# A four-layer conditioned transformer kernel: the first chunk's x loads go first, from two queues, and the position load goes behind the short loads

## Chip, cores and metric

One NeuronCore of one Trainium2 chip runs the kernel. The metric is device microseconds of one execution of the whole program. The core has TensorE (PE), VectorE (DVE), ScalarE (ACT), GpSimd (POOL) and SyncE (SP); SP issues nearly all DMA transfers, and in the changed kernel ACT issues two as well.

## What is computed

The input x is 8 sequences of 256 tokens of 512 features in float32. Four layers follow: L0 (adaptive RMS norm, attention with 8 query heads and one key/value head, rotary embedding from `pos_BxS`, gated MLP), L1 (adaptive layer norm, 16-head attention on normalised q and k, GELU MLP), L2 (windowed attention with a latent key/value projection) and L3 (eight small expert MLPs, norm, projection). Only the very beginning of L0 is touched here:

```python
def ada_rms(x, t, w, tw):
    n = x * rsqrt(mean(square(x), axis=-1, keepdims=True) + EPS)
    scale = t @ tw.T
    return n * (w * (1.0 + scale))[:, None, :]

def apply_rope(x, pos_ids):
    ang = pos_ids.astype(float32)[:, :, None] * inv_freq
    ...
h = ada_rms(x, time_emb, ln1_w, ln1_tw)
q, k, v = h @ Wq.T, h @ Wk.T, h @ Wv.T      # split into heads
q, k = apply_rope(q, pos_ids), apply_rope(k, pos_ids)
```

## The kernel before, in words

The 2048 tokens are four chunks (n = 0 to 3) of 512 tokens, two sequences each. Activations lie feature-major: `X[:, c, 512n:512n+512]` is feature block c (128 partitions) of chunk n. `ORDER` lists 12 (layer, chunk) items for attention, and MLPs and tail follow the same way. Each piece of work (a norm's statistics, a projection, a softmax) is a generator in `Plan`, cut into steps; the table `PLACE` gives each step a number, and `Plan.make` sorts all steps by it. Every engine then walks the same sorted list (`weights.steps`) and issues its own part of each step, so each engine's order is fixed by `PLACE`. Engines wait on semaphores, in order, and nothing overtakes a waiting instruction on its engine.

The beginning of the list, for chunk 0 of L0, is this:

- "start" (from `PLACE["once"][0]`): SP loads the column vectors `CV` (layer weights, biases, the rotary frequencies), the four x tiles of chunk 0 (one semaphore `s_x0[c]` each), the conditioning vectors `CT` and the identity `ident`. POOL writes three constants.
- "pos" (`PLACE["trig"][0]`): SP loads the 512 positions of the chunk, broadcast to 128 partitions, into a buffer of `FB` (semaphore `s_pos`).
- "angle" (`PLACE["trig"][1]`, place 2): DVE casts the positions to float, multiplies by the frequencies and rounds to whole turns: a CAST (L372) and three TENSOR_SCALAR (L375).
- "stats" (places 3 to 8): ACT squares the four x tiles into `T` (ACTIVATE `T<-X`), DVE adds the four squares (three TENSOR_TENSOR `T<-T`, L378), PE sums over partitions (`B<-few,T`), DVE scales (`R<-B`), POOL takes the power -0.5 (`R<-R,few`).
- "load ada" 0 (place 9) loads `Y` with 1 MB of modulation weights, "load rot" (10) brings the first weight tiles `ST` and the rotation matrix; "turns" (11) is the rest of the angle work on DVE; "final" (12, 17 to 28) multiplies x by the broadcast scale and splits it into a high and a low part, `HA`. The projections `B<-HA,W` on PE start when `HA` and the split weights `W` (POOL) are there.

DVE and ACT have each one wait ahead of their whole list: `e.wait_ge(*s_cv.of())`, on the landing of `CV` (L1440, and L1755 behind one tiny activation). DVE's first instruction then waits for the positions:

```python
elif kind == "angle":
    ...
    e.wait_ge(*s_pos.of(n))
    e.wait_ge(*fr.over(gu))
    e.tensor_copy(g, f.bitcast(I32)).then_inc(*d_trig.up(n, 0))
```

Calls go through the helper class `Engine`, so the profile shows helper lines: L360 is any matmul, L363 a transpose, L366 an activation, L372 a copy or cast, L375 tensor-scalar, L378 tensor-tensor, L381 scalar-tensor-tensor, L396 a DMA.

Of the kernel before, what the change touches and what calls it, by code (L numbers as in the profile page):

```python
# [27 lines left out]
AHEAD = 2  # L28
LAG = 1
PLACE = {  # L30
    "once": [1, 10, 39, 230, 845, 943, 1214, 2226, 9, 91, 323, 400, 436, 513, 572, 614, 678, 735, 804, 848],
    "ada": [13, 14, 15, 16, 123, 147, 177, 181, 395, 396, 407, 408, 433, 434, 473, 475, 484, 486, 494, 495, 545, 546,
# [140 lines left out]
    "trig": [0, 2, 11, 29, 43, 100, 102, 136, 288, 324, 344, 404, 589, 629, 661, 704],  # L173
    "xb": [1129, 1497, 1856, 2466, 1680, 2025, 2427, 2972],
    "out": [238, 239, 240, 241, 242, 243, 244, 245, 547, 548, 549, 550, 552, 554, 555, 556, 878, 879, 880, 881, 882,
# [248 lines left out]
def span(h):  # L424

    return slice(0, 512) if h == BOTH else slice(256 * h, 256 * h + 256)
# [539 lines left out]
def program(nc, xT, pos, condT, biasd, cols, consts, tab2, wpack, adaw, out):  # L966
    ctx = ExitStack()
    with ctx:
        def sb(name, shape, dt=F32):
            return ctx.enter_context(nc.sbuf_tensor(name, shape, dt))  # L970

        def tally(name, step=1):
            return Tally(ctx.enter_context(nc.semaphore(name)), step)

        X = sb("X", [128, 4, TOK])
# [51 lines left out]
        s_x0 = [tally(f"s_x0_{c}", 16) for c in range(4)]  # L1027
# [133 lines left out]
        def left(w):  # L1161

            y = weights.before[w]
            tl, key = wused[y] if y >= 0 else (p_ada, (-1,))
            return tl.of(*key)

        def written(w):

            return s_w[weights.slot(w)].of("store", weights.before[w])
# [580 lines left out]
                    dp.done(u, d_xl, n, m, h)  # L1750

        def scalar(e):
            e.wait_ge(*g_const.of(0))
            e.activation(R16[:, 0, 0, 0:1], mhalf[:, 0:1], ACT.Square)
            e.wait_ge(*s_cv.of())  # L1755
            e.wait_ge(*g_const.of(1))
            for step in weights.steps:
# [18 lines left out]
                elif kind == "nhi":  # L1776
                    i, c, f = a
# [129 lines left out]
                elif kind == "act":  # L1907
                    q, c, j, u, f = a
# [9 lines left out]
                elif kind == "ghi":  # L1918
                    q, c, j, f = a
# [88 lines left out]
        def sync(e):  # L2008
            for step in weights.steps:
                kind, a = step[0], step[1:]  # L2010
                if kind == "start":
                    e.dma_start(CV[:, :], cols).then_inc(*s_cv.up())
                    for c in range(4):
                        e.dma_start(X[:, c, 0:512], xT[:, c, 0:512]).then_inc(*s_x0[c].up())
                    e.dma_start(CT[:, 0, :, :], condT).then_inc(*s_ct.up())
                    e.dma_start(ident[:, :], consts[0]).then_inc(*s_id.up())
                elif kind == "load rot":
                    e.dma_start(rotm[:, :], consts[1]).then_inc(*s_rot.up(0))
                elif kind == "bias":
                    e.wait_ge(*p_adt.of(ADA_GROUPS - 1))  # L2020
                    e.dma_start(BI[:, :, :], biasd.rearrange("(a p) k -> p a k", p=128)).then_inc(*s_const.up("all"))
                elif kind == "load x":
                    e.dma_start(X[:, :, 512:TOK], xT[:, :, 512:TOK]).then_inc(*s_x.up())
                elif kind == "load ada":
                    i, = a
                    e.wait_ge(*p_ada.of(i - 1))
                    e.dma_start(Y[:, :, :], adaw[:, 2048 * i:2048 * i + 2048].rearrange("p (j k) -> p j k", j=4)).then_inc(*s_ad.up(i))
                elif kind == "load":
                    w, = a
                    i, c = weights.order[w], 512 * PIECE[weights.uses[w]]  # L2030
                    if i >= STAGES:
                        tl, key = stused[i - STAGES]
                        e.wait_ge(*tl.of(*key))
                    e.dma_start(ST[:, i % STAGES, :], wpack[:, c:c + 512]).then_inc(*s_st[i % STAGES].up(w))
                elif kind == "store":
                    w, = a
                    s = weights.slot(w)
                    e.wait_ge(*g_wlo.of(w))
                    e.dma_start(kept[PIECE[weights.uses[w]]], W[:, s, :, :].bitcast(F32)).then_inc(*s_w[s].up("store", w))
                elif kind == "fetch":  # L2040
                    w, = a
                    s, name = weights.slot(w), weights.uses[w]
                    e.wait_ge(*left(w))
                    e.wait_ge(*written(w))
                    first = weights.firsts[name]
                    e.wait_ge(*s_w[weights.slot(first)].of("store", first))
                    e.dma_start(W[:, s, :, :].bitcast(F32), kept[PIECE[name]]).then_inc(*s_w[s].up("fetch", w))
                elif kind == "tables":
                    e.wait_ge(*d_qk.of("q", 0, 3, 3))
                    e.dma_start(TR[:, 0, :], tab2[0]).then_inc(*s_tab.up(0))  # L2050
                    e.dma_start(TR[:, 1, :], tab2[1]).then_inc(*s_tab.up())
                elif kind == "swap":
                    k, fu, gu = a
                    f, g, d = fr.buf(fu), fr.buf(gu), HDIM[k[1]] // 2
                    e.wait_ge(*a_raw.of(*k))
                    e.wait_ge(*fr.over(gu))
                    if k in swap_before:
                        e.wait_ge(*s_swap.of(*swap_before[k]))
                    for x in range(0, 128, 2 * d):
                        e.dma_start(g[x:x + d, :], f[x + d:x + 2 * d, :]).then_inc(*s_swap.up("part"))  # L2060
                        e.dma_start(g[x + d:x + 2 * d, :], f[x:x + d, :]).then_inc(*s_swap.up(*k))
                elif kind == "pos":
                    n, fu = a
                    e.wait_ge(*fr.over(fu))
                    e.dma_start(fr.buf(fu).bitcast(I32),
                                pos[0:1, 512 * n:512 * n + 512].broadcast_to([128, 512])).then_inc(*s_pos.up(n))
                elif kind == "ladd":
                    n, m, h, u = a
                    sp = span(h)
                    e.wait_ge(*d_xl.of(n, m, h))  # L2070
                    e.dma_start(out[:, m, 512 * n:512 * n + 512][:, sp],
                                X[:, m, 512 * n:512 * n + 512][:, sp]).then_inc(*s_out.up(n, m, h))
            e.wait_ge(*s_out.of(NB - 1, 3, 1))

        for count in (tensor, vector, scalar, gpsimd, sync):
            count(Engine())
# [5 lines left out]
        @block.sync  # L2082
        def _(eng):
            sync(Engine(eng))
# [5 lines left out]
        @block.scalar  # L2090
        def _(eng):
            scalar(Engine(eng))
# [127 lines left out]
```

## Time and profile before

| | us |
|---|---|
| median of 3 runs | 1913.11 (1912.12 to 1913.13) |
| the profiled execution | 1912.22 |
| its span | 1910.4 |
| mean granted TensorE clock | 0.987 of full speed |
| PE busy | 1839.4 (96% of the span) |

The rows further down are lines of the profile's page and of answers from its trace. A line of a timeline gives the start in us, the duration, the engine, the line of the kernel, the operation, `out<-in`, and how often it occurs in a row; in brackets the idle time before it and what ended it. SPq is SP's queue of DMA issues; the duration there is that of the issue, not of the transfer. "us to landing" is the time from the issue to the completion that the semaphore shows.

### The profile page before, as it was taken

To read this page: it belongs to the slowest core of one execution; us is meant where nothing else is said; L and a number is where in the kernel's file an instruction comes from. 1 tells how busy PE (TensorE), PEld (TensorE's weight loads), DVE (VectorE), ACT (ScalarE), POOL (GpSimd) and SP (SyncE) were. 2 spreads that over 40 slices of the span, in tenths; PEclk is the share of its full clock that TensorE was granted. 3 is DMA by queue.
4 is the path that set the end of the run, shared out by engine and by line. 5 is a ranking of instruction groups with operands and counts; after the bars stand their busy time and mean duration, and the time that the engine had idled before them with its cause. 6 is when DMAs were issued, how large, how long until landed. Compare 5 with 4: busy or idle time off the path is not lost.

```text
span 1910.4 us, 35240 instructions
## 1 busy us (share of the span) xinstructions
PE 1839.4 (96%) x12840; PEld 1480.8 (78%) x12840; DVE 1130.7 (59%) x3224; ACT 1026.9 (54%) x2482; POOL 819.3 (43%) x1094
## 2 busy tenths in 40 slices
PE   5889999999999999999999999999999999989987
PEld 3678778888888888888788888878886878865565
DVE  5867445643553446543775488586475786476563
ACT  3553433532343445443566467477467765559875
POOL 4666662211112344233778565336443442244330
PEclk9999999999999999999999999999999999989989
DMA  7436787556445544445456534623532354422421
GB/s 246 140 122 215 255 292 257 191 196 221 156 171 176 187 167 144 166 160 183 141 172 226 180 144 144 208 102 126 206 122 85 132 193 172 165 83 90 127 73 56
DMA packets 98651, 314.76 MB, mean 165 GB/s; under 512 B 11568, under 2 KB 13232, under 8 KB 96944
## 3 DMA queue, kind: packets, MB, share of 16 engines
q1 hardware_dynamic: 98480, 312.52, 47.2%
q8 instruction: 103, 1.69, 0.4%
q14 instruction: 68, 0.56, 0.1%
HBM read 242.48 MB, written 66.58 MB: 162 GB/s over the span
## 4 chain that ended last, share of the span: by engine, by line
PE 85%; DVE 5%; ACT 4%; POOL 3%; DMA 2%; issue 2%; SPq 0%; DVEq 0%; POOLq 0%; ACTq 0%
PE B L360 78%; PE B L363 7%; POOL W L378 1%; ACT SS L366 1%; DMA ST<-in_wpack 1%; DVE T L378 1%; ACT GF L366 1%; DVE FB L381 1%; POOL W L375 1%; ACT L366 1%; POOL SS L375 1%; POOL FB L378 1%; DMA Y<-in_adaw 0%; DVE Y L378 0%; ACT FB L366 0%
## 5 line engine op out<-in xcount | busy, mean ns | idle before, releaser
L375 POOL TENSOR_SCALAR SS<-SS,NM 128x256 f32<-128x256 f32 (+1 forms) x640 | 298.7, 486 | 620.1 <-DVE NM L390 619.8
L360 PE MATMUL B<-HM,W 128*128 128x512 f32 x2304 | 532.1, 390 | 1.0 <-DVE HM L381 1.0
L360 PEld LDWEIGHTS B<-HM,W 128*128 128x128 f32 x2304 | 431.7, 188 | 91.8 <-DVE HM L381 1.8
L360 PE MATMUL B<-G,W 128*128 128x512 f32 x1536 | 381.6, 398 | 2.8 <-POOL W L378 2.4
L360 PEld LDWEIGHTS B<-G,W 128*128 128x128 f32 x1536 | 280.9, 188 | 64.2 <-issue 3.1
L366 ACT ACTIVATE SS<-SS,NM 128x256 f32<-128x256 f32 (+1 forms) x512 | 240.2, 472 | 72.8 <-DVE NM L384 72.4
L360 PE MATMUL B<-HA,W 128*128 128x512 f32 x864 | 221.0, 405 | 8.7 <-DVE HA L378 4.7
L360 PEld LDWEIGHTS B<-HA,W 128*128 128x128 f32 x864 | 161.7, 192 | 50.5 <-issue 8.7
L363 PE MATMUL B<-ident,SS 128*128 128x128 f32 x1152 | 166.7, 281 | 11.9 <-POOL SS L375 9.6
L378 POOL TENSOR_TENSOR R<-R,few 128x16 f32<-128x16 f32 (+2 forms) x57 | 120.7, 2121 | 126.2 <-DVE R L375 126.2
L363 PEld LDWEIGHTS B<-ident,SS 128*128 128x128 f32 x1152 | 133.8, 143 | 44.7 <-issue 13.4
L378 POOL TENSOR_TENSOR W<-ST,W 128x512 fp32r<-128x512 f32 x119 | 161.4, 1356 | 9.9
L378 DVE TENSOR_TENSOR G<-FB,G 128x512 fp32r<-128x512 f32 x128 | 102.0, 800 | 107.4 <-ACT G L366 106.9
L366 ACT ACTIVATE G<-FB 128x512 fp32r<-128x512 f32 x128 | 80.5, 631 | 139.0 <-DVE FB L378 135.9
L375 POOL TENSOR_SCALAR W<-ST 128x512 fp32r<-128x512 f32 x119 | 80.8, 679 | 156.2 <-PE B L360 107.8
L366 ACT ACTIVATE PT<-B 128x512 f32<-128x512 f32 x160 | 94.2, 590 | 98.1 <-PE B L363 97.6
L366 ACT ACTIVATE FB<-B 128x512 f32<-128x512 f32 (+2 forms) x148 | 86.1, 593 | 112.0 <-PE B L360 110.1
L378 DVE TENSOR_TENSOR FB<-FB,B 128x512 f32<-128x512 f32 x64 | 43.9, 686 | 163.2 <-PE B L360 150.7
L366 ACT ACT_TABLE_LOAD x107 | 137.3, 1283 | 3.9 <-DVE NM L384 1.3
L360 PE MATMUL B<-CX,W 128*128 128x512 f32 (+1 forms) x624 | 135.8, 375 | 0.0
L378 DVE TENSOR_TENSOR X<-X,B 128x512 f32<-128x512 f32 (+1 forms) x100 | 66.0, 664 | 117.7 <-PE B L360 117.6
L360 PEld LDWEIGHTS B<-CX,W 128*128 128x128 f32 x624 | 110.0, 188 | 21.2 <-issue 0.9
(111 smaller groups left out, 2647.2 us busy)
## 6 DMA issues: line engine op xcount, KB each, us to landing
W<-kept SPq DMA_DIRECT2D x357, 512.0 KB, 4.4
kept<-W SPq DMA_DIRECT2D x119, 512.0 KB, 4.9
ST<-in_wpack SPq DMA_DIRECT2D x139, 256.0 KB, 2.9
Y<-in_adaw SPq DMA_DIRECT2D x12, 1024.0 KB, 6.4
FB<-FB SPq DMA_DIRECT2D x52, 64.0 KB, 2.9
X<-in_xT SPq DMA_DIRECT2D x1, 3072.0 KB, 13.2
out_xT<-X SPq DMA_DIRECT2D x12, 256.0 KB, 3.8
FB<-in_pos SPq DMA_DIRECT2D x4, 256.0 KB, 5.0
```

What stands on the lines that cost most here:

```text
L360: return self.real.matmul(*a, **k) if self.real is not None else self
L363: return self.real.transpose(*a, **k) if self.real is not None else self
L366: return self.real.activation(*a, **k) if self.real is not None else self
L375: return self.real.tensor_scalar(*a, **k) if self.real is not None else self
L378: return self.real.tensor_tensor(*a, **k) if self.real is not None else self
L381: return self.real.scalar_tensor_tensor(*a, **k) if self.real is not None else self
```

## The change

The four x tiles of chunk 0 are issued first: tiles 0 and 2 by SP, ahead of `CV`, and tiles 1 and 3 by ACT, ahead of its first activation. Two numbers of `PLACE` are exchanged, so that "start" comes before "pos": the position load is issued behind `CV`, `CT` and `ident`. Each x tile keeps its own semaphore.

```diff
 PLACE = {
-    "once": [1, 10, 39, 230,
+    "once": [0, 10, 39, 230,
...
-    "trig": [0, 2, 11, 29, 43,
+    "trig": [1, 2, 11, 29, 43,
...
         def scalar(e):
+            for c in (1, 3):
+                e.dma_start(X[:, c, 0:512], xT[:, c, 0:512]).then_inc(*s_x0[c].up())
             e.wait_ge(*g_const.of(0))
...
                 if kind == "start":
+                    for c in (0, 2):
+                        e.dma_start(X[:, c, 0:512], xT[:, c, 0:512]).then_inc(*s_x0[c].up())
                     e.dma_start(CV[:, :], cols).then_inc(*s_cv.up())
-                    for c in range(4):
-                        e.dma_start(X[:, c, 0:512], xT[:, c, 0:512]).then_inc(*s_x0[c].up())
                     e.dma_start(CT[:, 0, :, :], condT).then_inc(*s_ct.up())
```

SP's queue at the start of the program, before (`FB<-in_pos` is the position load, `ST<-in_wpack` weight tiles, `rotm` the rotation matrix):

```order
L396 DMA FB<-in_pos 128x512
L396 DMA CV<-in_cols 128x123
L396 DMA X<-in_xT 128x512 x4
L396 DMA CT<-in_condT 128x128
L396 DMA ident<-in_consts 128x128
L396 DMA Y<-in_adaw 128x2048
L396 DMA ST<-in_wpack 128x512 x3
L396 DMA rotm<-in_consts 128x128
```

and with the change:

```order
L396 DMA X<-in_xT 128x512 x2
L396 DMA CV<-in_cols 128x123
L396 DMA CT<-in_condT 128x128
L396 DMA ident<-in_consts 128x128
L396 DMA FB<-in_pos 128x512
L396 DMA Y<-in_adaw 128x2048
L396 DMA ST<-in_wpack 128x512 x3
L396 DMA rotm<-in_consts 128x128
```

The position load has moved from the first row to the fifth, behind two x tiles, `CV`, `CT` and `ident`; two x tiles have left this queue.

ACT's first rows, before, each with the semaphores it waits for:

```order
L366 ACT_TABLE_LOAD
L366 ACTIVATE R<-few 128x1 [waits g_const]
L366 ACTIVATE T<-X 128x512 [waits s_x0_0,g_const,s_cv]
L366 ACTIVATE T<-X 128x512 [waits s_x0_1]
L366 ACTIVATE T<-X 128x512 [waits s_x0_2]
L366 ACTIVATE T<-X 128x512 [waits s_x0_3]
```

and with the change:

```order
L396 DMA X<-in_xT 128x512 x2
L366 ACT_TABLE_LOAD
L366 ACTIVATE R<-few 128x1 [waits g_const]
L366 ACTIVATE T<-X 128x512 [waits s_x0_0,g_const,s_cv]
L366 ACTIVATE T<-X 128x512 [waits s_x0_1]
L366 ACTIVATE T<-X 128x512 [waits s_x0_2]
L366 ACTIVATE T<-X 128x512 [waits s_x0_3]
```

ACT issues two x tiles ahead of its table load; the first square still waits for `CV` (s_cv).

DVE's first rows with the change; but for the line numbers of branches they are those of before:

```order
L372 CAST FB<-FB 128x512 [waits s_pos,g_const,s_cv]
L375 TENSOR_SCALAR FB<-FB,CV 128x512 [waits d_trig]
L375 TENSOR_SCALAR FB<-FB 128x512 [waits d_trig] x2
L378 TENSOR_TENSOR T<-T 128x512 [waits a_sq]
L378 TENSOR_TENSOR T<-T 128x512 [waits d_sq,a_sq] x2
L375 TENSOR_SCALAR R<-B 128x4 [waits p_var]
L381 SCALAR_TENSOR_TENSOR FB<-FB 128x512 [waits d_trig] x3
```

Nothing moved here: the cast of the positions, with its waits on s_pos and s_cv, is still DVE's first instruction, and the additions of the squares (`T<-T`) still stand behind it.

## Rows read from the trace of the kernel before

**Rows 1.** The page: busy time, and PE's busy tenths in 40 slices.
```profile
PE 1839.4 (96%) x12840; PEld 1480.8 (78%) x12840; DVE 1130.7 (59%) x3224; ACT 1026.9 (54%) x2482; POOL 819.3 (43%) x1094
...
PE   5889999999999999999999999999999999989987
```

**Rows 2.** The chain that ended last, 0 to 60 us: start, us, what.
```profile
1.63 3.98 DMA X<-in_xT
5.72 1.20 ACT T L366 x2
6.95 0.70 DVE T L378
...
9.38 1.86 PE B L360 x8
...
11.57 1.33 POOL R L378
...
14.06 1.91 PE B L360 x32
```

**Rows 3.** Timeline of DVE, 0 to 12 us.
```profile
4.97 0.43 DVE L372 CAST FB<-FB 128x512 f32<-128x512 int32 x1 [4.97 <-DMA CV<-in_cols]
5.44 0.48 DVE L375 TENSOR_SCALAR FB<-FB,CV 128x512 f32<-128x512 f32 x1
5.96 0.89 DVE L375 TENSOR_SCALAR FB<-FB 128x512 f32<-128x512 f32 x2
```

**Rows 4.** Timeline of ACT, 0 to 12 us.
```profile
0.72 1.28 ACT L366 ACT_TABLE_LOAD   x1 [0.72 <-PEq L2212]
...
5.72 2.59 ACT L366 ACTIVATE T<-X 128x512 f32<-128x512 f32 x4 [3.51 <-DMA X<-in_xT]
```

**Rows 5.** Timeline of SP's queue, 0 to 12 us.
```profile
0.72 0.39 SPq L396 DMA_DIRECT2D FB<-in_pos  x1
1.17 0.42 SPq L396 DMA_DIRECT2D CV<-in_cols  x1
1.63 1.85 SPq L396 DMA_DIRECT2D X<-in_xT  x4
3.53 0.43 SPq L396 DMA_DIRECT2D CT<-in_condT  x1
4.00 0.43 SPq L396 DMA_DIRECT2D ident<-in_consts  x1
4.48 0.43 SPq L396 DMA_DIRECT2D Y<-in_adaw  x1
```

**Rows 6.** DMA issues 0 to 40 us: KB each, median us to landing.
```profile
X<-in_xT SPq DMA_DIRECT2D x4, 256.0 KB, 4.3
Y<-in_adaw SPq DMA_DIRECT2D x1, 1024.0 KB, 6.7
FB<-in_pos SPq DMA_DIRECT2D x1, 256.0 KB, 3.9
...
ident<-in_consts SPq DMA_DIRECT2D x1, 64.0 KB, 4.5
...
CV<-in_cols SPq DMA_DIRECT2D x1, 61.5 KB, 3.8
```

**Rows 7.** DMA issues 17 to 18 us, columns as in rows 6.
```profile
ST<-in_wpack SPq DMA_DIRECT2D x1, 256.0 KB, 2.6
```

**Rows 8.** Stretches: busy of PE, PEld, DVE, ACT, POOL; clock, DMA share, GB/s.
```profile
1.50:4.00 2.50, 0.00 (x0) 0.00 (x0) 0.00 (x0) 0.70 (x2) 0.00 (x0) 1.00 0.68 146
5.00:8.50 3.50, 0.00 (x0) 0.00 (x0) 3.13 (x6) 2.45 (x4) 0.00 (x0) 1.00 1.06 382
```

**Rows 9.** Stretches 30 to 150 us, columns as in rows 8.
```profile
30.00:60.00 30.00, 21.80 (x140) 15.05 (x139) 19.84 (x51) 15.48 (x44) 20.70 (x25) 0.91 0.89 323
60.00:100.00 40.00, 35.03 (x282) 25.98 (x281) 33.26 (x87) 23.63 (x64) 26.39 (x34) 0.94 0.20 63
100.00:150.00 50.00, 45.45 (x261) 36.87 (x260) 30.17 (x66) 24.83 (x59) 31.23 (x38) 0.93 0.42 138
```

More of the change, by code:

```diff
@@ L30 @@
 PLACE = {
-    "once": [1, 10, 39, 230, 845, 943, 1214, 2226, 9, 91, 323, 400, 436, 513, 572, 614, 678, 735, 804, 848],
+    "once": [0, 10, 39, 230, 845, 943, 1214, 2226, 9, 91, 323, 400, 436, 513, 572, 614, 678, 735, 804, 848],
     "ada": [13, 14, 15, 16, 123, 147, 177, 181, 395, 396, 407, 408, 433, 434, 473, 475, 484, 486, 494, 495, 545, 546,
@@ L172 @@
         3712, 3713],
-    "trig": [0, 2, 11, 29, 43, 100, 102, 136, 288, 324, 344, 404, 589, 629, 661, 704],
+    "trig": [1, 2, 11, 29, 43, 100, 102, 136, 288, 324, 344, 404, 589, 629, 661, 704],
     "xb": [1129, 1497, 1856, 2466, 1680, 2025, 2427, 2972],
```

## The prediction

> **What bounds the kernel now.** I began with the page. PE is busy for 1839.4 of 1910.4 us, and its only thin slice is the first (5 tenths in 48 us) [rows 1]. So a delay ahead of PE's first large matmuls moves the end by its own size, unless something later takes it up, and there is not much that could be gained in the middle. The change touches only the first 10 us, so everything is decided by what ends last there.
>
> The chain of waits [rows 2] tells it: the x tiles land; two squares on ACT from 5.72 us; then DVE adds squares from 6.95; PE sums from 9.38; POOL takes the power at 11.57; PE multiplies the modulation weights at 14.06. Up to 6.95 us the chain runs through x and ACT. But the timelines of DVE and ACT show a second chain that ends almost at the same time. DVE starts its cast of the positions at 4.97, released by the landing of `CV`, and its three following operations end at 5.96 + 0.89 = 6.85 us [rows 3]. The second square ends at 5.72 + 1.20 = 6.92 [rows 2]. The first addition starts at 6.95. The reader should see that **two things arrive together**: DVE is free at 6.85 and the squares are there at 6.92. An earlier x alone could win at most 0.1 us, as the position block stands ahead of the addition on the same in-order engine.
>
> **The change part by part.**
>
> *x first, from two queues.* SP issues transfers about 0.47 us apart (0.72, 1.17, 1.63) [rows 5]. x tile 0 was issued at 1.63, the last some 1.4 us later; now all four are issued at about 0.72 to 1.2 us, half of them by ACT. By the median of 4.3 us to landing [rows 6] they land at 5.0 to 5.5 us instead of 5.9 to 7.4. The trace of before shows no ACT issue; I take SP's 0.47 us for each, so ACT's table load (1.28 us from 0.72) [rows 4] ends near 2.95. ACT's first square waits until 5.4 us for other reasons (next part), so this lies under a wait with over 2 us to spare and costs nothing. Without that cover, if an ACT issue took over 1.5 us, the excess would land on the squares, which even then have slack behind the position block.
>
> *`CV` one place later.* It goes from the issue at 1.17 to the one at 1.63. With its 3.8 us to landing it arrives at 5.43 instead of 4.97 [rows 5, 6]; with x tiles in front of it I allow 6.4 (1.63, `ident`'s 4.5 us, and 0.3 more). Both ACT and DVE wait for it before anything else. ACT then squares from 5.4 to 6.4 us, four squares in 2.59 us [rows 4], and the second is done by 7.7 at the latest. That is hidden as long as DVE comes free later than 7.7, which the next part says.
>
> *Positions five places back.* This is the term that counts. SP's queue now reads x, x, `CV`, `CT`, `ident`, positions, so the issue is the sixth of 0.47 us: at 0.72 + 5 x 0.47 = 3.05 us instead of 0.72. How long it then takes to land the trace doesn't show, so I bound it:
>
> - Below: the shortest landing of a transfer of this size in a quiet stretch, 2.6 us [rows 7], gives 5.65 us.
> - Its own landing of before, 3.9 us with nothing ahead of it [rows 6], gives 6.95 us.
> - The x tiles, one of which was issued at just this moment into a full queue, took 4.3 us (7.35), and `ident`, the last of the same set of transfers before `Y`, took 4.5 us (7.55) [rows 6].
> - Above: the set in front of `Y` is the same eight transfers in both kernels, 1.5 MB. Before, it was complete when `ident` landed, 4.00 + 4.5 = 8.5 us [rows 5, 6]. If the two queues win nothing, the positions, now last of the set, land then.
>
> The DMA engines moved only 146 GB/s from 1.5 to 4 us and 382 GB/s, fully busy, from 5 to 8.5 us [rows 8]. At 382 the 1.5 MB take 3.9 us; begun at 1.5 and with a tail of about 1 us, that makes 6.4, and more if the slow start stays. I take **7.5 us**, nearest to the x and `ident` rows, because those were issued into the same crowd.
>
> For the landing of one 256 KB transfer the row of the positions gives 3.9 us. The Trainium skill (DMA: Bandwidth & Descriptors, Anatomy of one DMA — SWDGE (gpsimd) path) fits about 2.0 us plus bytes over 436e3 for GpSimd's path, so 2.6 us here; the quiet row agrees with it, the rows at the start of the program do not. By the page the sum below would be +0.6 us and not +2.5.
>
> The block on DVE (cast to last rounding step) takes 6.85 - 4.97 = 1.88 us [rows 3] and nothing in it changes. It starts at 7.5 and ends at 9.4; the first addition starts then instead of at 6.95. By 9.4 all four squares are done, so the three additions follow as before. Term: 9.4 - 6.95 = **+2.45 us**; by the bounds 5.65 and 8.5 it is +0.6 and +3.4.
>
> *What is queued behind.* Behind the cast on DVE stand the additions; PE's first matmul, then DVE's scaling, POOL's power and, on in-order POOL, every weight split, wait for them in turn. PE's modulation matmuls wait behind the statistics too. `Y` is issued about 0.95 us earlier (two issues fewer ahead on SP) and was there at 4.48 + 6.7 = 11.2 us [rows 5, 6], before PE came to it at 14.06 [rows 2]: earlier or later by a microsecond, it changes nothing. The weight tiles' reloads wait for POOL's splits and move along. So from 9.38 us on, the program is the old one, 2.45 us later, and with PE at 96% I find nothing downstream that would take it up.
>
> **Sum.** 1912.22 (the profiled execution; its span 1910.4 and 1.8 outside it) + 2.45 = 1914.7. The median of the runs shown lies 0.9 above the profiled one, so against 1913.11 I expect **1915.6 us**, +0.13%. About 0.2%, 3.8 us, is what a measurement of this kernel tells from no change, so this is "same", leaning to slower.
>
> **Rivals.**
>
> *A. The delay is small.* The positions land in about 2.6 us as the quiet row has it, or later waits take up part of the delay: +0.6 to +1.9 us, 1913.7 to 1915.0. For it: the slow first microseconds of rows 8 held the positions and `CV` themselves, so their successors may fare better. Against it: the engines were full from 5 us on. Chance 0.15.
>
> *B. The positions share the engines with `Y`.* `Y` (1 MB) is issued right behind them, at about 3.5 us. If its data mix with theirs, they land as late as `Y`: 3.53 + 6.7 = 10.2 us, the block ends at 12.1, +5.15 us: 1918.3, slower by over 0.2%. The point from which it decides is a landing after 8.9 us. Against it: `ident`, issued just ahead of `Y`, landed at 8.5 and `Y` at 11.2. Chance 0.09. The Trainium skill (DMA: Bandwidth & Descriptors, Queues, rings and completion order) says that one engine consumes the descriptors of a queue in ring order, which speaks against the mixing; the two landings agree.
>
> *C. The clock's low stretches move, and it ends faster.* From 30 to 150 us the granted clock averages 0.91, 0.94 and 0.93 over 30, 40 and 50 us [rows 9]: 2.7 + 2.4 + 3.5 = 8.6 us of full clock are missing. PE is partly idle just there, waiting. If the shift of 2.45 us kept all of them away, the time would be 1913.1 + 2.45 - 8.6 = 1907.0; over 6.3 of the 8.6 would have to go for faster by over 0.2%. Against it: three runs lie within 1.0 us, so these stretches come in every run. Chance 0.03; the same the other way round (more low clock, past +3.8 in all) 0.03.
>
> *D. The change does what it says and pays.* If x were what is waited for, the squares would be there up to 0.3 us earlier. DVE's row order excludes more: the cast waits for `CV`, now later, and for the positions, which would have to land 1.9 us after their issue to start it at 4.97. No row is that short. Less than 0.2% in any case. I give it 0.02.
>
> **How the numbers follow.** Forecast 0.68, A 0.15, B 0.09, C 0.06 in two halves, D 0.02. Slower: B, C's slower half: 0.12. Faster: 0.03. Same: 0.85. The range starts where A's low end meets the spread of the runs (1913.7 - 0.8 = 1912.9) and ends at the forecast's upper bound of +3.4 with a spread of 1.1 on top, 1917.6; B, C and some of D lie outside.
>
> **What would show it.** In the new profile: x tiles landed by about 5.5; ACT's first square at 5.4 to 6.4, released by `CV` and no longer by x; DVE's cast at about 7.5, released by the position load; the chain of waits starting with SP's queue and `FB<-in_pos`, not `X<-in_xT`; the first addition at 9.4 and PE's first matmul at 11.8; the squares done before DVE comes to them. A cast before 6.5 us shows A, one after 8.9 B. If PE's first matmul is 2 to 3 us late and the end is not, something later absorbed it, and my step "nothing downstream takes it up" was wrong.

## The result and the profile after

| | median us | ratio to before, 95% interval |
|---|---|---|
| before, in the first comparison | 1912.61 (6 runs) | |
| the change, first comparison | 1918.34 (6 runs) | 1.0035 (1.0025 to 1.0046) |
| the change, second comparison | 1917.00 (12 runs; before 1912.95 in 29) | 1.0021 (1.0012 to 1.0031) |
| the change, third comparison | 1917.33 (8 runs; before 1912.69 in 13) | 1.0032 (1.0019 to 1.0045) |

The change makes the kernel slower, by 4.0 to 6.7 us in the three comparisons if the ratio is taken times 1913 us. The recorded ratio is not the quotient of the two medians; the medians themselves differ by 5.7, 4.1 and 4.6 us. Ratios of 1.0025 to 1.0031 lie in all three intervals, that is 4.8 to 5.9 us. The forecast was 1915.6 us, range 1912.9 to 1917.6, with 85% on "within 0.2%", and it added 2.45 us to before. The first median lies above the range; the other two lie inside it, but their excess over before is above 2.45 us too. Single runs of before spread from 1907.4 to 1917.5 us once there were many of them, much wider than the three that were known.

The page of the first profiled execution of the changed kernel (1920.84 us) answers to [rows 1]; its span is 1919.0:

```profile
PE 1847.3 (96%) x12840; PEld 1486.9 (77%) x12840; DVE 1130.5 (59%) x3224; ACT 1027.0 (54%) x2482; POOL 815.6 (43%) x1094
...
PE   4899999999999999999999999999999999989997
```

PE is busy in the first slice for 4 tenths instead of 5, and for 7.9 us more in total. The work is the same; the mean granted clock of this execution was 0.983 against 0.987. The extra busy time goes with the clock and not with the change: a second profile of the changed kernel (after_again), at a clock of 0.988, has PE busy for 1838.4 us. The first execution, at 1920.84 us, is the slowest of its six, so I read the beginning from it and the cost from the medians.

The chain that ended last, answering to [rows 2] (start, us, what):

```profile
3.05 5.81 DMA FB<-in_pos
8.99 0.44 DVE FB L372
...
10.43 0.43 DVE FB L375
10.86 0.61 DVE T L378
...
13.20 1.85 PE B L360 x8
```

It no longer starts with an x load. It goes along SP's issues to the load of the positions, which takes 5.81 us, and through DVE's cast into the additions. DVE's own timeline, answering to [rows 3], says the same with the releaser in brackets:

```profile
8.99 0.43 DVE L372 CAST FB<-FB 128x512 f32<-128x512 int32 x1 [8.99 <-DMA FB<-in_pos]
9.45 0.49 DVE L375 TENSOR_SCALAR FB<-FB,CV 128x512 f32<-128x512 f32 x1
9.97 0.89 DVE L375 TENSOR_SCALAR FB<-FB 128x512 f32<-128x512 f32 x2
10.77 1.48 DVE L378 TENSOR_TENSOR T<-T 128x512 f32<-128x512 f32 x2
```

DVE idles for 8.99 us until `FB<-in_pos` lands; before, it idled 4.97. ACT's timeline, answering to [rows 4]:

```profile
0.72 0.90 ACTq L396 DMA_DIRECT2D X<-in_xT  x2
1.65 1.28 ACT L366 ACT_TABLE_LOAD   x1 [1.65 <-PEq L2214]
...
6.01 2.19 ACT L366 ACTIVATE T<-X 128x512 f32<-128x512 f32 x4 [2.86 <-DMA CV<-in_cols]
```

ACT issues its two x tiles in 0.90 us, loads its table, and waits for `CV`, not for x. All four squares are done at 6.01 + 2.19 = 8.20 us, more than 2 us before the additions start. SP's queue, answering to [rows 5], and the landings, answering to [rows 6] (KB, median us to landing):

```profile
3.05 0.43 SPq L396 DMA_DIRECT2D FB<-in_pos  x1
3.53 0.43 SPq L396 DMA_DIRECT2D Y<-in_adaw  x1
```

```profile
Y<-in_adaw SPq DMA_DIRECT2D x1, 1024.0 KB, 8.2
X<-in_xT ACTq DMA_DIRECT2D x2, 256.0 KB, 4.1
X<-in_xT SPq DMA_DIRECT2D x2, 256.0 KB, 3.9
FB<-in_pos SPq DMA_DIRECT2D x1, 256.0 KB, 5.8
...
CV<-in_cols SPq DMA_DIRECT2D x1, 61.5 KB, 4.4
```

x lands early, as meant, after 3.9 to 4.1 us from 0.72 and 1.17. The positions, issued at 3.05, take 5.8 us. What the DMA engines did in the meantime is in the stretches, columns as in [rows 8] (the last two numbers are the DMA engines' busy share and GB/s):

```profile
1.50:4.00 2.50, 0.00 (x0) 0.00 (x0) 0.00 (x0) 1.49 (x2) 0.00 (x0) 1.00 0.90 280
4.00:5.50 1.50, 0.00 (x0) 0.00 (x0) 0.00 (x0) 0.00 (x0) 0.00 (x0) 1.00 1.04 354
5.50:7.00 1.50, 0.00 (x0) 0.00 (x0) 0.00 (x0) 0.99 (x2) 0.00 (x0) 1.00 0.50 106
7.00:8.50 1.50, 0.00 (x0) 0.00 (x0) 0.00 (x0) 1.19 (x3) 0.00 (x0) 1.00 0.97 377
```

From 1.5 to 5.5 us 280 x 2.5 + 354 x 1.5 = 1231 thousand bytes move, nearly all of the 1243 thousand of x, `CV`, `CT` and `ident`. So what runs next is the load of the positions, and from 5.5 to 7 us **the DMA engines move only 106 GB/s**, with 1 MB of `Y` issued behind it in the same queue. The same stretch in the other two profiles of the changed kernel, after_again and after_third:

```profile
5.50:7.00 1.50, 0.00 (x0) 0.00 (x0) 0.00 (x0) 0.59 (x2) 0.00 (x0) 1.00 0.98 128
5.50:7.00 1.50, 0.00 (x0) 0.00 (x0) 0.00 (x0) 1.01 (x2) 0.00 (x0) 1.00 1.01 152
```

The low rate is in all three. The busy share of 0.50 is not: in the other two the engines are counted as fully busy and still move only 128 and 152 GB/s. Before, the same load stood in the 146 GB/s of 1.5 to 4 us [rows 8]; what it cost there the run rows_before shows.

### The profile page after: what moved, and what is told of

Same layout as the page of the kernel before. It is cut to its first block, busy times and chain, and to the rows that moved or that the text cites. A ratio compares the mean times of both kernels' runs of the same rounds, so it can differ in the third digit from the quotient of the medians.

```text
span 1919.0 us, 35240 instructions
## 1 busy us (share of the span) xinstructions
PE 1847.3 (96%) x12840; PEld 1486.9 (77%) x12840; DVE 1130.5 (59%) x3224; ACT 1027.0 (54%) x2482; POOL 815.6 (43%) x1094
## 4 chain that ended last, share of the span: by engine, by line
PE 86%; DVE 4%; ACT 3%; POOL 3%; DMA 2%; issue 1%; SPq 0%; POOLq 0%; DVEq 0%; ACTq 0%
PE B L360 79%; PE B L363 8%; ACT SS L366 1%; DMA ST<-in_wpack 1%; POOL W L378 1%; DVE FB L381 1%; DVE T L378 1%; ACT GF L366 1%; ACT L366 1%; DMA Y<-in_adaw 1%; POOL W L375 0%; POOL FB L378 0%; POOL SS L375 0%; ACT FB L366 0%; DMA FB<-in_pos 0%
```

## The experiments

In the table "PE" is the start of PE's first matmul in the profile (9.38 us before, 13.20 with the change), "late" its distance from 9.38, and "time" the ratio's excess over 1, times the median of before, with its 95% interval. Every start is that of one profiled execution. Three more kernels were run once each and stand further down.

| kernel | PE | late | time against before |
|---|---|---|---|
| the change, three profiles | 13.20, 13.15, 13.75 | 3.8, 3.8, 4.4 | +6.7, +4.0, +6.1 |
| delay_dve | 13.57 | 4.2 | +4.2 (2.5 to 5.9) |
| delay_long | 18.86 | 9.5 | +8.6 (6.1 to 11.1) |
| pos_first | 12.24 | 2.9 | +2.9 (1.1 to 4.6) |
| angle_late | 9.71 | 0.3 | +1.0 (-0.8 to 2.5) |
| pos_rows | 11.54 | 2.2 | +2.1 (0.2 to 3.8) |
| sp_only | 14.91 | 5.5 | +4.4 (2.7 to 5.9) |
| best | 8.22 | -1.2 | -0.6 (-2.5 to 1.1) |

**delay_dve: what does a late start cost?** The kernel before, with fills of buffers that are unused at that point:

```diff
         def vector(e):
             e.wait_ge(*s_cv.of())
             e.wait_ge(*g_const.of(1))
+            e.memset(GF[:, :, :], 0.0)
+            e.memset(SS[:, 0, :, :], 0.0)
+            e.memset(SS[:, 1, :, :], 0.0)
```

> The kernel before, with three DVE fills of unused buffers (4096 elements per partition in all) ahead of the cast of the positions, and nothing else. By the rate of the cast (512 elements in 0.43 us) they take about 3.4 us; the profile gives the size. It moves the first addition and everything behind it by that size. Theory 1 (a late start costs its own length): the time rises by the delay, about +3.4 us. Theory 2 (a late start also costs TensorE clock or other waits later): more than the delay, about 1.7 times it, +5 to +6 us, as the change itself cost 6.7 us (ratio 1.0035) for PE's first matmul 3.8 us late.

Measured: 1916.93 us, ratio 1.0022 (1.0013 to 1.0031). DVE's timeline:

```profile
5.59 1.76 DVE L369 MEMSET GF<- 128x2048 f32 x1 [5.59 <-DMA CV<-in_cols]
7.52 0.91 DVE L369 MEMSET SS<- 128x1024 f32 x1 [0.16 <-issue]
8.59 0.91 DVE L369 MEMSET SS<- 128x1024 f32 x1 [0.16 <-issue]
9.42 0.36 DVE L372 CAST FB<-FB 128x512 f32<-128x512 int32 x1
```

The first matmul is 4.2 us late and the time rises by 4.2: theory 1, and 1.7 times the delay (7.1 us) is outside the interval. Of the 4.2 us, 0.6 come from DVE's start at 5.59 instead of 4.97, which the fills do not explain; for the cost of a late start it makes no difference.

**delay_long** adds six more such fills:

```diff
+            e.memset(SS[:, 2, :, :], 0.0)
+            e.memset(PT[:, 0, :, :], 0.0)
+            e.memset(PT[:, 1, :, :], 0.0)
+            e.memset(PT[:, 2, :, :], 0.0)
+            e.memset(V[:, 0, :, :], 0.0)
+            e.memset(V[:, 1, :, :], 0.0)
```

> The kernel before with fills of unused buffers ahead of DVE's cast, about 8.8 us of them (4.2 us before). Theory 1 (a late start costs its own length): PE's first matmul at about 18 us and the time about 8.7 us above before, ratio 1.0045. Theory 2 (part is taken up later, or part is added by clock): clearly off that, under +6.5 or over +11 us.

Measured: 1922.44 us (5 runs), ratio 1.0045 (1.0032 to 1.0058), for a delay of 9.5 us, somewhat more than I had reckoned. Within the intervals a late start costs its own length: nothing later absorbs it, and nothing multiplies it.

**pos_first: the second queue without the late positions.** The two numbers of `PLACE` go back:

```diff
-    "once": [0, 10, 39,
+    "once": [1, 10, 39,
...
-    "trig": [1, 2, 11,
+    "trig": [0, 2, 11,
```

> The change with the two numbers of PLACE put back: positions first on SP, then x tiles 0 and 2, CV, CT, ident; x tiles 1 and 3 from ACT. Theory 1 (the late positions are the whole loss): the cast starts when CV lands (issued at 2.1 instead of 1.17), 6 to 6.5 us, the first addition at 8 to 8.4, so +1 to +1.5 us against before, and most of the loss is gone. Rival (the second queue or CV's place is the loss): the time stays near the change's, +4 us or more.

Measured: 1915.56 us, ratio 1.0015 (1.0006 to 1.0024). The cast starts later than I expected, and the landings say why:

```profile
8.03 0.43 DVE L372 CAST FB<-FB 128x512 f32<-128x512 int32 x1 [8.03 <-DMA CV<-in_cols]
```

```profile
X<-in_xT ACTq DMA_DIRECT2D x2, 256.0 KB, 5.6
...
FB<-in_pos SPq DMA_DIRECT2D x1, 256.0 KB, 5.0
...
CV<-in_cols SPq DMA_DIRECT2D x1, 61.5 KB, 5.9
```

The cast waits for `CV`, not for the positions. `CV` is issued at 2.1 behind the positions and two x tiles and takes 5.9 us, and even ACT's x tiles take 5.6 instead of 4.1. So the late positions are not the only way to lose: **here what runs beside or behind the broadcast load lands late**. No run has this order with a load that is not broadcast, so how much of the 5.9 us is the broadcast and how much the transfers ahead is not shown. Theory 1's "most of the loss is gone" failed: of the 3.8 us by which PE starts late, 2.9 remain. Whether the time is better than the change's can't be told either, as the interval reaches to +4.6 us.

**angle_late: the position block out of the way on DVE.** The step "angle" of chunk 0 goes from place 2 to 7, which puts the cast and the three operations after it behind the additions:

```diff
-    "trig": [1, 2, 11,
+    "trig": [1, 7, 11,
```

> The change, and the position block on DVE (cast to rounding, 1.88 us) moved behind the three additions, under PE's sums of the squares (1.85 us): place 7 instead of 2. Theory 1 (DVE's order behind the position load is the loss): the additions start behind the second square at about 7.2 us, PE's first matmul at 9.5 to 9.7, within 0.5 us of before; the time is within 1 us of before. Rival (the x path itself has become slow, or ACT's queue costs elsewhere): still +3 us or more.

Measured: 1914.24 us, ratio 1.0005 (0.9996 to 1.0013).

```profile
7.28 2.29 DVE L378 TENSOR_TENSOR T<-T 128x512 f32<-128x512 f32 x3 [7.28 <-ACT T L366]
9.50 0.43 DVE L372 CAST FB<-FB 128x512 f32<-128x512 int32 x1
...
11.59 0.16 DVE L375 TENSOR_SCALAR R<-B 128x4 f32<-128x4 f32 x1 [0.22 <-PE B L360]
```

The additions now start at 7.28, behind the second square, and the block runs under PE's sums; DVE's scaling at 11.59 waits 0.22 us for PE. PE starts at 9.71, within 0.3 us of before. The same loads in the same order, the same late positions (6.4 us to landing here), and the loss is gone from the start. So the loss of the start is made by DVE's order behind that load.

**pos_rows: why do the positions land late?** The host lays them out as 128 equal rows, a layout without arithmetic, and the load reads one row per partition:

```diff
-                                pos[0:1, 512 * n:512 * n + 512].broadcast_to([128, 512])).then_inc(...)
+                                pos[:, 512 * n:512 * n + 512]).then_inc(...)
```

> The change, with the positions laid out by the host as 128 rows, so that each partition reads its own 2 KB instead of all reading the same. Theory A (the positions land late, 5.8 us after their issue, because a load broadcast from one row moves at about 100 GB/s): they land as the x tiles do, 4.0 to 4.4 us after the issue, the cast starts at 7.2 to 7.5, and the time is 1.5 us below the change's. Rival B (they are only queued behind five transfers): the landing stays at 5.5 us or more and the time does not move.

Measured: 1915.45 us, ratio 1.0011 (1.0001 to 1.0020).

```profile
7.33 0.43 DVE L372 CAST FB<-FB 128x512 f32<-128x512 int32 x1 [7.33 <-DMA FB<-in_pos]
```

```profile
FB<-in_pos SPq DMA_DIRECT2D x1, 256.0 KB, 4.1
```

```profile
5.50:7.00 1.50, 0.00 (x0) 0.00 (x0) 0.00 (x0) 0.99 (x2) 0.00 (x0) 1.00 1.02 323
```

The same 256 KB at the same place in the queue land after 4.1 us instead of 5.8, and from 5.5 to 7 us the engines move 323 GB/s instead of 106 to 152. Theory A holds; the place in the queue (B) is not what made it 5.8.

**rows_before** makes the same edit in the kernel before (one execution).

> The kernel before with the positions as 128 own rows, nothing else. In it the load of the positions was the first on the queue and landed after 3.9 us, CV behind it after 3.8, where CV issued first landed after 2.7 and x tiles issued first after 3.4. Theory (the broadcast load is slow by itself and holds back what is queued behind it): positions land after 3.0 to 3.5 us, CV after 3.0 to 3.3, the first square starts at 5.0 to 5.3 instead of 5.72. Rival (the first microseconds are slow whatever is loaded): landings of 3.8 to 4 us as before, first square at 5.7.

```profile
X<-in_xT SPq DMA_DIRECT2D x4, 256.0 KB, 3.6
...
FB<-in_pos SPq DMA_DIRECT2D x1, 256.0 KB, 2.8
...
CV<-in_cols SPq DMA_DIRECT2D x1, 61.5 KB, 2.9
```

```profile
4.85 1.24 ACT L366 ACTIVATE T<-X 128x512 f32<-128x512 f32 x2 [2.63 <-DMA X<-in_xT]
6.43 1.28 ACT L366 ACTIVATE T<-X 128x512 f32<-128x512 f32 x2 [0.34 <-DMA X<-in_xT]
```

```profile
1.50:4.00 2.50, 0.00 (x0) 0.00 (x0) 0.00 (x0) 0.70 (x2) 0.00 (x0) 1.00 0.77 222
```

Positions after 2.8 us (3.9 before), `CV` after 2.9 (3.8), x after 3.6 (4.3), first square at 4.85 instead of 5.72, PE's first matmul at 8.73 instead of 9.38. Each is one trace, but delay_dve and delay_long begin with the loads of before, and theirs lie with it: positions 4.2 and 4.1, `CV` 3.9 and 3.9, x 4.4 and 4.4. So this one load made the start of the kernel before slower, by about 0.65 us at PE. It is not all of the slow first stretch: 222 GB/s from 1.5 to 4 us is more than 146, and still less than the 382 of later. Its one time, 1913.36 beside 1912.83, is too little to see 0.6 us.

**rows_16** (one execution): the change with 16 equal rows, each read by 8 partitions.

```diff
-                                pos[0:1, 512 * n:512 * n + 512].broadcast_to([128, 512])).then_inc(...)
+                                pos[:, 512 * n:512 * n + 512].unsqueeze(1).broadcast_to([16, 8, 512])).then_inc(...)
```

> The change, positions laid out as 16 equal rows, each read by 8 partitions. From one row they landed after 5.8 us, from 128 own rows after 4.1. If the slowness comes from many reads of the very same bytes at once, 16 rows take away most of it: 4.1 to 4.6 us. If any read of a row by several partitions is slow, it stays at 5.3 us or more.

The landing took 5.3 us, just at the border of the two cases. It is below the 5.8 and 6.4 us of the changed kernel's profiles and above the 4.1 of own rows, and from 5.5 to 7 us 244 GB/s moved, between the two again. One trace doesn't decide it: whether the cost is in reading the same bytes at once or in any shared row stays open.

**sp_only: the change without ACT's part.**

```diff
         def scalar(e):
-            for c in (1, 3):
-                e.dma_start(X[:, c, 0:512], xT[:, c, 0:512]).then_inc(*s_x0[c].up())
...
-                    for c in (0, 2):
+                    for c in range(4):
```

> The change without ACT's part: SP issues all four x tiles first, then CV, CT, ident, positions. Each of CV and the positions is issued 0.95 us later than with the change. Theory 1 (only the positions' landing counts, and a queue is served in its order): the positions land about 1 us later than with the change, the cast starts at 9.9 to 10.0, PE's first matmul at 14.1 to 14.2, +4.8 us against before. Rival (the engines are the limit, and issue order within a microsecond does not matter): the cast starts within 0.3 us of the change's 8.99 and the time is the change's.

Measured: 1917.68 us, ratio 1.0023 (1.0014 to 1.0031).

```profile
10.69 0.43 DVE L372 CAST FB<-FB 128x512 f32<-128x512 int32 x1 [10.69 <-DMA FB<-in_pos]
```

```profile
X<-in_xT SPq DMA_DIRECT2D x4, 256.0 KB, 3.3
...
FB<-in_pos SPq DMA_DIRECT2D x1, 256.0 KB, 6.6
...
CV<-in_cols SPq DMA_DIRECT2D x1, 61.5 KB, 3.8
```

The direction was right, the size too small: the cast starts 1.7 us after the change's, not 1 us; why the positions lost 0.75 us beyond the later issue I did not find out. But `CV`, issued 0.95 us later, landed at about the same time as in the change (ACT starts at 6.43, against 6.01 and, in the change's second profile, 6.41), as the x tiles from one queue landed after 3.3 us and not after 4. What two queues win for x and `CV` is at most the issue time. The Trainium skill says the same (DMA: Bandwidth & Descriptors, Issuing engines are not separate DMA queues): issuing from several engines saves only the time to initiate.

**best** puts `CV` first on SP, x tiles 0 and 1 on ACT, 2 and 3 on SP, the positions behind them from 128 rows, and the block on DVE at place 7.

```diff
             for c in (0, 1):
                 e.dma_start(X[:, c, 0:512], xT[:, c, 0:512]).then_inc(*s_x0[c].up())
...
                     e.dma_start(CV[:, :], cols).then_inc(*s_cv.up())
                     for c in (2, 3):
                         e.dma_start(X[:, c, 0:512], xT[:, c, 0:512]).then_inc(*s_x0[c].up())
```

> All that the runs so far speak for: CV first on SP, then x tiles 2 and 3; x tiles 0 and 1 from ACT; positions behind them and from 128 own rows; the position block on DVE behind the additions (place 7). Theory 1: CV lands at about 4.6 us, x tile 0 too, ACT squares from 4.7 to 5.0, PE's first matmul at 8.4 to 8.7, that is 0.7 to 1.0 us earlier than before: +-0 within what can be timed, at best -1 us. Rival (the start of the DMA engines, not the order, sets the first landing): squares no earlier than 5.7 us and PE's first matmul at 9.4.

Measured: 1912.65 us beside 1912.95, ratio 0.9997 (0.9987 to 1.0006).

```profile
3.76 0.63 ACT L366 ACTIVATE T<-X 128x512 f32<-128x512 f32 x1 [0.62 <-DMA X<-in_xT]
5.03 1.67 ACT L366 ACTIVATE T<-X 128x512 f32<-128x512 f32 x3 [0.64 <-DMA X<-in_xT]
```

```profile
X<-in_xT ACTq DMA_DIRECT2D x2, 256.0 KB, 3.4
...
CV<-in_cols SPq DMA_DIRECT2D x1, 61.5 KB, 2.7
```

`CV` issued first lands after 2.7 us, the first square starts at 3.76, PE at 8.22, 1.2 us earlier than before. That is too little for the timing: level with before, not shown faster.

**best_bcast** (one execution) is best with the one-row broadcast.

> The best kernel with the positions broadcast from one row again. Theory: what is ahead of the positions does not notice, so squares and additions start as in best (3.8 and 5.8 us); the positions land at 8.5 to 9 us instead of 6.85, so the cast, which stands behind the additions (free at 8.0), starts at 8.5 to 9, DVE's scaling 0.5 to 1.0 us later than in best. Rival: no landing changes, since only the queue counts: scaling at 10.1 as in best.

```profile
6.24 2.28 DVE L378 TENSOR_TENSOR T<-T 128x512 f32<-128x512 f32 x3 [6.24 <-ACT T L366]
9.45 0.43 DVE L372 CAST FB<-FB 128x512 f32<-128x512 int32 x1 [0.92 <-DMA FB<-in_pos]
...
11.23 0.15 DVE L375 TENSOR_SCALAR R<-B 128x4 f32<-128x4 f32 x1
```

The positions land late again (6.4 us), the cast waits for them at 9.45, and the scaling starts at 11.23 instead of 10.10, a little more than expected; the additions start 0.45 us later too, which I had not expected. PE's next step waits for that scaling. Its single time, 1910.07 beside 1912.83, is lower than best's median and shows only the spread of single runs.

**after_again, after_third: the change itself, timed twice more.**

> The changed kernel as it is, timed again beside more runs of the kernel before, since its first comparison rests on six runs of each. A pure delay of 4.2 us cost +4.2 us (ratio 1.0022, interval 1.0013 to 1.0031). Theory 1 (the change costs the 3.8 us by which PE's first matmul is late, and the rest of the first 6.7 us was spread of the runs): +3.8 us, ratio about 1.0020, interval reaching below 1.0025. Theory 2 (the change costs something beside that delay, such as the second queue or clock): again +6 us or more, ratio 1.0030 and up.

> The changed kernel a third time. PE's first matmul is 3.8 us late in both profiles so far, but the two comparisons gave ratios of 1.0035 (1.0025 to 1.0046) and 1.0021 (1.0012 to 1.0031). Theory 1 (the cost is that delay and no more): about +3.8 us again, ratio 1.0020, at most 1.0025. Theory 2 (some 1 to 3 us come on top): 1.0028 or more.

The second comparison gave what theory 1 said (1.0021, +4.0 us). The third gave 1.0032 (1.0019 to 1.0045), above theory 1's "at most 1.0025". Its profile, though, shows a longer delay: the cast starts at 9.54, PE at 13.75, 4.4 us late.

```profile
9.54 0.43 DVE L372 CAST FB<-FB 128x512 f32<-128x512 int32 x1 [9.54 <-DMA FB<-in_pos]
```

So the landing of the positions differs from one execution to the next (casts at 8.99, 8.94 and 9.54), and the delay with it. That covers 3.8 to 4.4 us. By the ratios the first comparison has 2.9 us and the third 1.7 us on top, by the medians 1.9 and 0.3 us. Whether this is real is not settled: the second comparison has next to none, and sp_only, with a longer delay, has none. The mean granted clock does not show it: 0.985 in the third comparison's runs of both kernels.

## Why the prediction was wrong, point by point

*What bounds the start* was right: two chains ended together at 6.9 us, and an earlier x could win nothing while the position block stood ahead of the additions on DVE. ACT's issues took 0.90 us, its table load ended at 2.93 against the 2.95 I reckoned, and both lay under a wait. `CV` released ACT at 6.01, inside 5.4 to 6.4; the squares were done in time. The chain did start with the position load.

*The step that failed is the term of the positions' landing*: "I take 7.5 us, nearest to the x and `ident` rows", with 8.5 as upper bound. It was 8.86 to 8.99, and 9.5 once. The cast started at 8.99, the first addition at 10.77 in DVE's timeline, 3.8 us late instead of 2.45. The error was in how I read two rows. The positions' own 3.9 us looked like the landing of a lone transfer, and I took x and `ident` as the harder cases. And the 146 GB/s of 1.5 to 4 us looked like a slow start of the engines, common to whatever comes first. The first was the broadcast load and the second was so in part: with own rows it lands after 2.8 us in the same place and the stretch moves 222 GB/s (rows_before). With own rows the cast of the changed kernel starts at 7.33, near the 7.5 of the forecast, PE's first matmul is 2.2 us late and the time +2.1 us (0.2 to 3.8), where the forecast had +2.45 (pos_rows). My bound from the completed set of transfers failed with it: before, that load ran while the other transfers were still being issued; now it drained last, with nothing of x left beside it, at 106 to 152 GB/s. "If the two queues win nothing, the positions, now last of the set, land then" was no upper bound.

*Nothing downstream takes it up* was right, to what can be timed: delays of 4.2 and 9.5 us cost 4.2 and 8.6. With the measured delay instead of the forecast one, the sum would have been 1913.1 + 3.8 = 1916.9, at the border of 0.2%. With the same 1.1 us of spread on top the range would have ended at 1918.0, and at 1918.6 with the 4.4 us of the third profile; so the first median of 1918.34 is not covered by the delay of its own profile. The range was too narrow for another reason: it took the spread of three runs, 1.0 us, for that of the kernel, and many runs spread over 10.

*Rivals.* A did not come. B's own mark, a cast after 8.9, was met in all three profiles (8.99, 8.94, 9.54). Its mechanism as written, positions that land as late as `Y`, did not come: they landed at 8.86 and `Y` at 3.53 + 8.2 = 11.7. But `Y`'s data did move beside theirs. From 1.5 to 8.5 us the four stretches add up to 1956 thousand bytes, 450 thousand more than the eight transfers ahead of `Y` have, and the positions had not landed yet. Rows 8 had this already: 365 thousand bytes from 1.5 to 4 and 1337 thousand from 5 to 8.5 us are more than the 1505 thousand of the set, so `ident`'s landing at 8.5 did not speak against `Y` running beside it. pos_rows, with `Y` issued at the same moment, shows that `Y` alone does not make the landing late (4.1 us); whether it adds to the broadcast's time was not tested, as no run issues `Y` later. C did not come: the granted clock of the timed runs averages 0.984 to 0.985 for the change and 0.985 for before. The clock does go with the spread of single runs, though: of 78 timed runs of before in the later comparisons, the 24 at a mean clock of 0.987 average 1911.9 us and the 14 at 0.983 or below 1914.9 us. D's exclusion by DVE's order held. The page's rule of 2.0 us plus bytes over 436e3 (the Trainium skill, DMA: Bandwidth & Descriptors, Anatomy of one DMA) gives an estimate of 2.6 us for the positions; own rows on an empty queue took 2.8 (rows_before), so the rule, which the page fits for GpSimd's path, comes near the size here and misses the broadcast.

## What to carry to other kernels

Before you move a transfer, ask what its landing is made of: a load that is slow by itself can be cheap as the first of the queue (here 0.65 us at PE) and costly as the last, where an engine waits for it alone (3.8 us). Move the instruction that waits along with the load: with the consumer left first on an in-order engine, an earlier x could not be used and a later load stopped everything. Take the spread of a kernel from more than three runs before you set a range in tenths of a per cent.

## What the runs showed of the hardware

A 256 KB load that 128 partitions read from one 2 KB row took 3.9 to 6.6 us to land, and the stretch in which it ran moved 106, 128 and 152 GB/s in the three profiles of the changed kernel, at busy shares of 0.50, 0.98 and 1.01. The same bytes from 128 rows landed in 2.8 to 4.1 us, with 323 GB/s in that stretch. `CV` (61.5 KB) landed after 2.7 and 3.1 us as the first load (best, best_bcast), after 2.9 us behind the positions from own rows (rows_before), and after 3.8 us behind the broadcast (before) and 5.9 us behind the broadcast and two x tiles (pos_first). The data of `Y` moved while a load issued ahead of it in the same queue had not landed. Timed runs of one kernel spread over 10 us of 1913 (0.5%), so that even 12 against 29 runs leave an interval of +-1.8 us.
